# A two-layer network on one core: VectorE's operands in the state-space part, and the order of small weights in DRAM

## What is computed

```python
# first layer's experts: INTER 176, E 14; second layer's: F 96, E 16
g = silu(einsum('td,efd->etf', xf, wg)); u = einsum('td,efd->etf', xf, wu)
o = einsum('etf,edf->etd', g * u, wd)                    # "down" weights wd
# second layer, state-space block: D_INNER 3072 channels, 48 heads of 64, state 128
z, xc, B, C, dt = split(rms(x) @ in_proj_w.T)
xp = concatenate([conv_state, xc])                       # 3 columns ahead of the sequence
xc = silu(conv_b + sum(conv_w[:, k] * xp[:, :, k:k + s] for k in range(4)))
h  = exp(A * dt) * h + B[..., None] * x_t                # step by step over the tokens
y  = einsum('bhnp,bhn->bhp', h, C) + D_param * x_t
y  = rms(y) * silu(z)
x  = x + y @ out_proj_w.T + experts(...)
```

## Time and profile before

| | us |
|---|---|
| median of 3 runs | 3403.2 |
| lowest and highest | 3400.52 and 3411.67 |
| the profiled execution | 3401.37 |
| its span in the profile | 3399.3 |
| busy in the span: PE | 2803.6 |
| busy in the span: DVE, ACT, POOL | 2334.0, 2002.7, 1807.7 |
| `ssm`, from its first DMA to the end | about 1667 |

### The profile page before, as it was taken

The page is one execution under the profiler, slowest core; times in us unless marked ns, Lnnn a source line. Parts: engine busy times, 40 slices in busy tenths (PEclk is TensorE's granted clock), DMA queues, the critical chain, the costliest instruction groups (busy, mean ns, idle before and its releaser), DMA issues. The chain is left out here.

```text
span 3399.3 us, 55677 instructions
## 1 busy us (share of the span) xinstructions
PE 2803.6 (82%) x16828; PEld 2069.8 (61%) x16828; DVE 2334.0 (69%) x5175; ACT 2002.7 (59%) x4381; POOL 1807.7 (53%) x1365
## 2 busy tenths in 40 slices
PE   4679999977299475468649999999999999999998
PEld 2356666656189343257537767677676767767675
DVE  3346666664356367455448888888888888888886
ACT  3334554423255344355337777777777777777776
POOL 2211111127100344233248888888888888888887
PEclk8779999989699667689769999999999999999999
DMA  4244444436633633455466656565655655556563
GB/s 137 64 129 156 151 163 158 162 137 232 152 114 124 238 119 99 104 186 179 142 192 194 182 178 188 173 192 175 209 178 173 191 176 184 183 179 186 160 195 107
DMA packets 309968, 555.61 MB, mean 163 GB/s; under 512 B 47920, under 2 KB 158768, under 8 KB 309552
## 3 DMA queue, kind: packets, MB, share of 16 engines
q1 hardware_dynamic: 295856, 514.28, 48.9%
q0 software_dynamic: 13824, 37.77, 3.5%
HBM read 435.25 MB, written 116.66 MB: 162 GB/s over the span
## 5 line engine op out<-in xcount | busy, mean ns | idle before, releaser
L2514 POOL TENSOR_TENSOR mm<-mt,cb 128x1024 f32<-128x1024 f32 x192 | 462.1, 2407 | 243.8 <-ACT mt L2473 243.8
L2456 ACT ACTIVATE mt<-a_wide,a_tok 128x128 f32<-128x128 f32 x1536 | 486.0, 388 | 13.7 <-POOL mm L2514 13.0
L2586 DVE SCALAR_TENSOR_TENSOR cv<-bank,taps,cv 128x509 f32<-128x509 f32 (+2 forms) x576 | 428.7, 744 | 13.7
L2391 PE MATMUL bank<-yz,wo 128*128 128x512 f32 x768 | 361.9, 594 | 0.0
L59 PE MATMUL bank<-f,wi 128*128 128x512 f32 x768 | 321.0, 418 | 12.0 <-DMA wi<-ssm_wi_split 12.0
L61 PE MATMUL bank<-f,wi 128*128 128x512 f32 x768 | 304.1, 396 | 0.0
L60 PE MATMUL bank<-f,wi 128*128 128x512 f32 x768 | 303.7, 395 | 0.0
L2364 PE MATMUL bank<-mm,x_tok 128*64 128x128 f32 x3072 | 210.8, 279 | 63.3 <-POOL mm L2514 44.5
L2364 PEld LDWEIGHTS bank<-mm,x_tok 128*64 128x64 f32 x3072 | 164.7, 137 | 146.7 <-POOL mm L2514 145.6
L2535 POOL TENSOR_TENSOR yz<-y,zs 128x512 f32<-128x512 f32 x192 | 245.4, 1278 | 15.1
L2531 POOL TENSOR_TENSOR y<-t 128x512 f32<-128x512 f32 x192 | 245.2, 1277 | 1.5 <-DVE t L2633 1.2
(11 more groups left out here) (446 smaller groups left out, 7506.8 us busy)
## 6 DMA issues: line engine op xcount, KB each, us to landing
wi<-ssm_wi_split SPq DMA_DIRECT2D x192, 512.0 KB, 4.2
a_wide<-a_scratch SPq DMA_DIRECT2D x192, 512.0 KB, 5.8
l_fw<-ffn_split SPq DMA_DIRECT2D x72, 768.0 KB, 4.6
ea<-ea_scratch SPq DMA_DIRECT2D x384, 128.0 KB, 3.1
wo<-ssm_wo_scaled SPq DMA_DIRECT2D x192, 128.0 KB, 3.1
ssm_wi_split<-l_s_out SPq DMA_DIRECT2D x24, 512.0 KB
sorted_scratch<-fr_zeros SPq DMA_DIRECT2D x4, 3072.0 KB
ey_x<-sorted_scratch SPq DMA_DIRECT2D x96, 128.0 KB, 2.3
```

Source lines behind the costliest of these rows:

```text
L2391: i = pe.matmul(bank[:, OUT + m, :], wo[:, g % R, m * P:(m + 1) * P], yz[:, g % 2], start=t == 0, stop=t == LAST)
L2456: i = act.activation(mt[:, h, chunk(j)], a_wide[:, g % R, h, chunk(j)], ACT.Relu, bias=a_tok[:, s * NJ + j, 2 * t + h:2 * t + h + 1], scal ...
L2514: pl.tensor_tensor(mm[:], mt[:], cb[:, s * NJ:(s + 1) * NJ, :].rearrange("p j t -> p (j t)") .unsqueeze(1).broadcast_to([P, 2, TS]), ALU.m ...
L2586: dve.scalar_tensor_tensor(cv[:, a:TS], bank[:, X, 0:TS - a], taps[:, t, k:k + 1], cv[:, a:TS], ALU.mult, ALU.add).then_inc(ph["tap"], 1)
```

## The change

Three things.

1. In `ssm`, DVE no longer has an operation with two SBUF tensors as inputs. The boundary term, now `first` and with the bias in it, is made by POOL, as one small operation in each of six beats for each half of a step; ACT's `cv` leaves out the first three columns; DVE makes them with one operation out of the PSUM bank, `taps` and `first`. At the end of a step the output is multiplied in place in PSUM and then added to `acc` straight after it, ahead of the beat's convolution; `proj` is gone, and PE's next use of the output banks waits for the addition.
2. `vec` is copied in the first block of the program, DRAM to DRAM, into an array that lies as `ssm` reads it; `ssm` loads that first. SP's start of `ssm` has another order: the weights and decays of the first two tiles come before `dec` and `chain`, and DVE waits for `chain` only before its first `scan`.
3. The down rows of both mixtures (22 pieces of 112 KB, 12 of 128 KB) are copied DRAM to DRAM during the first seven steps of `layer0`, five to a step, behind loads of `fw` on SP's queue. `experts` loads them in two DMAs of 88 partitions with 14 KB each, behind the fourth and the seventh piece of `raw`; `experts1` in two halves of 96 partitions with 8 KB each, and its splitting goes by halves too.

The core of the diff:

```diff
                 sp.dma_start(tab[:], table).then_inc(ph["table"], 16)
+                sp.dma_start(vec_dram, mamba[:, :, MP_VEC:MP_ST].rearrange("t p c -> p t c")).then_inc(swdge["vec"], 16)
...
+                def order_down(n):
+                    if n < N_DOWN0:
+                        h, r = n // (N_DOWN0 // 2), n % (N_DOWN0 // 2) * 8
+                        sp.dma_start(down_drams[0][h, r:r + 8], moe0[n, 0:E0 * 8, 2 * KD * P:MLP].rearrange("(e f) d -> f e d", e=E0))\
+                            .then_inc(swdge["ordered0"], 16)
+                    elif n < N_DOWN0 + N_DOWN1:
...
                             hidden_weights(f, t)
+                            if t in (1, 3, 5, 6, 7):
+                                order_down(f * 5 + (1, 3, 5, 6, 7).index(t))
...
@@ experts @@
-                        sp.dma_start(wd_raw[r:r + Q, :, i // NI2, :],
-                                     moe0[i, 0:E0 * Q, 2 * KD * P:MLP_W].rearrange("(e f) d -> f e d", e=E0))\
...
+                        if i == 3:
+                            sp.wait_ge(swdge["ordered0"], NI * 16)
+                        if i in (3, 6):
+                            h = i // 6
+                            sp.dma_start(wd_raw[:, h], down_dram[h]).then_inc(ph[f"down{h}"], 16)
...
@@ experts1 @@
-                    for i in range(NI):
-                        sp.dma_start(wd_raw[i * Q:(i + 1) * Q],
-                                     moe1[i, :, 2 * KD * P:MLP_W].rearrange("(e f) d -> f e d", e=NE)).then_inc(ph["down"], 16)
+                    sp.wait_ge(swdge["ordered1"], NI * 16)
+                    for h in range(2):
+                        sp.dma_start(wd_raw[:, half(h)], down_dram[:, half(h)]).then_inc(ph[f"down{h}"], 16)
+                        for i in range(h * RG // 2, (h + 1) * RG // 2):
+                            sp.dma_start(place(i), moe1[i, :, 0:2 * KD * P]).then_inc(ph[f"raw{i}"], 16)
...
@@ ssm, SP @@
+                sp.wait_ge(swdge["vec"], 16)
+                sp.dma_start(vec[:], vec_dram).then_inc(ph["vec"], 16)
                 inputs(0)
                 weights_in(0)
-                sp.dma_start(vec[:], m_dram[:, :, MP_VEC:MP_ST].rearrange("t p c -> p t c")).then_inc(ph["vec"], 16)
                 log_decay(0)
+                weights_in(1)
+                log_decay(1)
+                since_start(0)
                 decays(0)
                 sp.dma_start(chain[:, 0], m_dram[:, :, MP_ST:MP_W].rearrange("t p c -> p t c")).then_inc(ph["init"], 16)
-                for k in range(-1, N + 1):
+                for k in range(0, N + 1):
...
@@ ssm, ACT @@
-                    act.activation(cv[:], bank[:, X, :], ACT.Identity, bias=taps[:, t, 4:5], scale=taps[:, t, 3:4])\
+                    act.activation(cv[:, 3:TS], bank[:, X, 3:TS], ACT.Identity, bias=taps[:, t, 4:5], scale=taps[:, t, 3:4])\
...
@@ ssm, POOL, at the end of a beat @@
+                    if 0 <= t - HALF - 1 < 6 and s + 1 < G:
+                        edge(s + 1, 0, t - HALF - 1)
+                    if 0 <= t - 1 < 6 and 0 < s < G:
+                        edge(s, 1, t - 1)
...
@@ ssm, DVE @@
-                    dve.tensor_tensor(cv[:, 0:3], cv[:, 0:3], edge[:, t, :], ALU.add).then_inc(ph["tap"], 1)
+                    dve.wait_ge(ph["edge"], 2 * s + (t >= HALF) + 1)
+                    dve.scalar_tensor_tensor(cv[:, 0:3], bank[:, X, 0:3], taps[:, t, 3:4], first[:, t, :],
+                                             ALU.mult, ALU.add).then_inc(ph["tap"], 1)
...
-                    dve.tensor_tensor(proj[:], bank[:, OUT:OUT + KD, :], yr[:].unsqueeze(1).broadcast_to([P, KD, TS]), ALU.mult)\
...
-                    dve.tensor_tensor(acc[:], acc[:], proj[:], ALU.add).then_inc(ph["sum"], 1)
+                    o = bank[:, OUT:OUT + KD, :]
+                    dve.tensor_tensor(o, o, yr[:].unsqueeze(1).broadcast_to([P, KD, TS]), ALU.mult).then_inc(ph["scaled"], 1)
+                    done(dve, "scaled", s)
+                    done(dve, "acc", s, 16)
+                    dve.tensor_tensor(acc[:], o, acc[:], ALU.add).then_inc(ph["evac"], 1)
```

More of the change, by code:

```diff
@@ L116, in program @@
         ident = col("ident")
+        swdge = {n: ctx.enter_context(nc.semaphore(n)) for n in
+                 [f"group{r}" for r in range(4)] + [f"put{r}" for r in range(4)] + [f"{n}{a}{j}" for n in ("in", "back") for a in range(2) for j in range(NJ)] + ["vec", "ordered0", "ordered1"] +
+                 [f"sent{b}{r}" for b in range(B) for r in range(4)]}
+        down_drams = (nc.dram_tensor("down0_scratch", (2, IN0 // 2, E0, D), F32, kind="Internal").ap(),
+                      nc.dram_tensor("down1_scratch", (IN1, NE, D), F32, kind="Internal").ap())
+        vec_dram = nc.dram_tensor("vec_scratch", (P, NCT, 12), F32, kind="Internal").ap()
         with nc.Block(no_gpsimd_drain=True) as block:
@@ L1914, in _ @@
                 def _(act):
[L1915 to L1916 removed]
                     for i in range(NI):
+                        if i in (0, RG // 2):
+                            h = i // (RG // 2)
+                            act.wait_ge(ph[f"down{h}"], 16)
+                            act.activation(wd_hi[:, half(h)], wd_raw[:, half(h)], ACT.Copy).then_inc(ph["down_high"], 1)
                         act.wait_ge(ph[f"raw{i}"], 16)
@@ L2667, in _ @@
                         state_part(k - 2)
-                    if has(e) and e % NCT == LAST:
-                        add(e // NCT)
         ph.clear()
```

126 lines of the change are left out of this document (61 added, 65 removed).

## The result

The changed kernel takes 3303.2 us (median of 4 runs, 3299.61 to 3303.34), the kernel before 3402.55 beside it (3400.52 to 3411.67): a ratio of 0.970, 95% interval 0.968 to 0.972. The forecast was 3295 in a range from 3272 to 3329. The profiled execution has a span of 3301.5 us against 3399.3, so 97.8 us are to be found again. The table has the length of each stretch, from the first DMA of one to the first of the next by SP's queue; the last two by PE's output projections.

The account below looks back on a forecast made before the run. In `ssm`, half the time, PE was nearly full but waited shortly for POOL's `mm` each beat; in the mixtures' weights PE stood still. Terms 32 + 9 + 18 + 8 + 28 + 19 - 5 - 1 = 108 us gave 3295, range 3272 to 3329.

Parts of the forecast that it names:

- The beat: In `ssm`, the loop of two beats gets 0.37 us shorter, the beat 8.17 becomes 7.99: 32 us, from 0 to 38.
- the beat does not move: Rival, chance 0.12: in `ssm` DVE's new operation waits for POOL too, or another link takes over at once; 3327 us.
- PE becomes full: Rival, chance 0.08: step ends cost only ACT's root; 38, 25 and 17 us instead of 32, 18 and 9; 3274 us.
- The operations on `edge`: In `ssm`, two groups per step leave DVE; 7 groups gain some 1 us, 7 gain 0.3: 9 us, bounds 0 and 17.
- The step ends: In `ssm`, 7 step ends each lose 2.5 us put down to the addition from SBUF: 18 us, bounds 0 and 25.
- The start: Start of `ssm`: DVE began 8.5 us after `cv` was ready, when `chain` had landed; gain 8 us, bounds 0 and 9.
- The second mixture: Its weights, 4.7 MB at 300 GB/s, end at 1443 instead of 1461.4: 19 us, bounds 10 and 23.
- The first mixture: Its weights, 8.3 MB at 300 GB/s, end at 908 instead of 938: 28 us taken, bounds 17 and 34.
- the weights do not come faster: Rival, chance 0.10: new large loads move slowly, others queue behind; mixtures 17 and 10 us, copies cost 16; 3326 us.
- The copies in the first layer: In `layer0`, 34 DRAM to DRAM copies behind loads of `fw`, most passing in the gap: -5 us, bounds 0 and -51.
- The slower rival: Rival, chance 0.02: copies in `layer0` hold up `fw`, 34 x 5.2 = 177 us fall on PE; 3467 us.
- The copy of `vec`: In the program's first block, the added copy costs time: -1 us, bounds 0 and -4.

Follow-up runs that it names:

- parting by expert: The changed kernel with each of the two loads of the first mixture's down rows parted into seven, one for each expert: 3292.59 us, ratio 0.968.

## Why the prediction came out

- **The beat (32 us, measured 35.0).** Right in mechanism and size. The small addition waited for POOL because of its two SBUF operands; with one in PSUM it takes 209 to 224 ns, inside the bounds 150 and 240. The beat is 7.99, as forecast, and the rival "the beat does not move" is out. Of the rival "PE becomes full" the condition came true, PE being the limit of the steady beats now, and with it its 17 us for the operations on `edge`; its 38 and 25 us did not.
- **The operations on `edge` (9 us with bounds 0 and 17, measured 17.5).** Mis-sized by half, just beyond its bound. The step that failed is the division into 7 groups at 1 us and 7 at 0.3: DVE's 0.82 us of idle time was counted as cover, and for the groups at the step's end ACT's root as well. All 14 groups cost 1.25 us on average, some 1.4 in the middle of a step and 1.0 at its end.
- **The step ends (18 us, measured 5.3).** The excess of 6.46 us per end was divided between ACT's root (3.9) and the addition (2.5). The addition accounts for 0.8. Of the rest, 0.7 is in the first of the four beats, directly behind the step's edge group (8.87 us between `scores` where a steady beat has 8.18), and 1.2 in the last, where the small addition behind the large one takes 1.00 us: time of the two terms above, counted here under another name. So this error and the one above nearly cancel: 27 predicted for the two, 22.8 measured. A stretch's excess tells the sum of its causes, not their shares.
- **The start (8 us, measured 8.8; 8 to 10 by the experiment).** Right, and the wait for `chain` is its cause.
- **The second mixture (19 us, measured 19.5, some 22 by the experiment).** Right.
- **The first mixture (28 us, measured 19.6, bounds 17 and 34).** The term of the sum that was mis-sized is the speed: 300 GB/s for all 8.3 MB, taken from `raw` with 2 KB rows. The down rows come in rows of 14 KB; while they move, it is 198 to 224 GB/s. The prediction had the last bytes at 3 + 27.6 = 30.6 us behind the first load and 1 us for the last split; measured it is 37.8 and 4.9, since the down rows stand ahead of most of `raw`, and DVE was fed unevenly and finished 13 loads in one go. (Its own working, 938 less 908, gives 30 us; it took 28.) So the mechanism of the rival "the weights do not come faster", large loads that move slowly with the others queued behind them, came true in the first mixture, near its 17 us, and not in the second. The Trainium skill's rule on the number of engines (DMA: Bandwidth & Descriptors, "Why a DMA increments its semaphore by 16 and not by 1"; 88 partitions make 11) was estimated at 4 us. The runs agree in direction, with 2.3 and 2.7; it explains a third of the gap between 28 and 19.6; parting by expert gave 5.6, of which the length of the rows is shown for 2.4 to 3.5. I had put it beside the sum and not into it; with it the sum would have been 3299.
- **The copies in the first layer (-5 us).** Neither confirmed nor refuted: PE's wait for `l_fw` went from 19.3 to 16.7 us, where an increase was forecast. The slower rival (177 us) is out. The length of the first layer goes with the granted clock more than with anything that was changed in it.
- **The copy of `vec` (-1 us, bounds 0 and -4).** Outside its bounds where it can be measured: DVE starts 7 us later. It moves 3072 pieces of 48 bytes, and was costed by its bytes. It stands ahead of the loads with which the first layer starts.

By the table at the top the forecast of 108 us was missed by -1.6 in the beats, +0.8 at the start, -8.4 and +0.5 in the two mixtures' weights, -1.9 in the first layer and +0.4 in the stretches that nothing touched: -10.2, so 97.8. The cancelling errors inside the beats don't show in that; there the number was more right than its reasons, by luck. That the two stretches of the first layer and of the blocks come out near is in part luck too, as one profile can't place the first to better than 10 us.

The rule behind the two-operand term is in the Trainium skill (SBUF — State Buffer, "SBUF: two separate sides"): a port pair shared by VectorE and GpSimd is taken for a whole instruction, and a VectorE operation with two SBUF inputs needs it, against a GpSimd operation that reads SBUF. The trace agrees: 220 against 601 ns for the small one, 1.22 against 2.86 us for the addition, with one operand exchanged in each.

## What to carry to other kernels

A VectorE operation with two SBUF operands beside a busy GpSimd costs what is left of GpSimd's instruction, however few columns it has (here 3 and 24): look for a small operation with a large spread of durations, and give it one operand from PSUM. When a load is made contiguous, ask how long its rows become and on how many partitions it stands; the fewest DMAs are not the fastest here, and whatever is loaded behind a slow one waits too. Read apart when the last bytes land and what is left to do then. When an excess of several causes is divided up, undo one of them at a time before believing the shares.

## What the runs showed of the hardware

- While two loads of 1.26 MB with rows of 14 KB on 88 partitions are under way, 230 GB/s move by full DMA share; with the same bytes in rows of 1 KB it is 293 to 312. Fourteen times as many DMAs took 5.6 us less.
- A copy from DRAM to DRAM in 48-byte pieces, issued in 0.70 us, delays the loads behind it by 7 us.
- One of the three chips is 1.7% slower with the kernel before (3460.25 against 3401 and 3403). In the profiles of its four kernels it is above all the second mixture's blocks that are longer, 324 to 328 us against 270 to 273, and the first layer a little (the first mixture starts at 879.9 to 898.4 against 869.7 to 892.3); everything in `ssm` has the same length as elsewhere. The cause wasn't looked for.
